# Target one-hots stored in DRAM in one pass of a graph kernel and read back in two later ones

## The chip, the core and the metric

The kernel runs on one core of a Trainium2 chip. Its engines are TensorE (PE, matrix products), VectorE (DVE), ScalarE (ACT), GpSimd (POOL) and SyncE (SP), which here only issues transfers. The metric is the time of one execution in device microseconds, as the median of several runs; lower is better.

## What is computed

Four graph layers run one after the other over 12,500 nodes with 32 features and 212,500 edges sorted by target. Each takes a layer norm and a ReLU of x and adds its sums to x:

```
h = relu(layernorm(x));  x += segment_sum(h_rel[src, type] * w, dst)          # layer 0
h = relu(layernorm(x));  x += relu(h@W0 + T1@W1 + (2*prop(T1) - h)@W2 + b)    # layer 1, T1 = prop(h)
h = relu(layernorm(x));  x += attention messages summed over dst              # layer 2
h = relu(layernorm(x));  x += segment_sum(h[src], dst) / max(degree, 1)       # layer 3
prop(v) = segment_sum(w_hat * v[src], dst)
```

So there are five sums over edges. The code numbers them 0, 1, 2 (the two `prop` of layer 1), 3 (attention) and 4 (the mean of layer 3), and a source's row must reach each edge in all of them.

## The kernel before

**Two ways to fetch a row.** Edges lie in 208 groups of 1,024. In the first way GpSimd gathers the rows of a group with eight indirect DMAs of 128 rows each (`gather_rows`, L709), VectorE weighs them and compares their targets with a window of 80 nodes (`weigh_group`, `compare`, L1997), TensorE sums them by the resulting one-hot (`multiply_group`, L1105), and VectorE adds the window to `big` (`add_group`, L1569), after which the slot (one of four) is free for the next gather (L1563). Sums 0 and 3 do all 208 groups this way.

**The second way** avoids the gather. While sum 0 runs, blocks of four groups are sorted by source into 49 buckets of 256 nodes with up to 128 slots each. In sums 1, 2 and 4, part of the edges goes as blocks: 26, 26 and 34 of them (`BLOCKS`). The text calls these sums pass 1, pass 2 and pass 4. What is left for gathers is 104, 104 and 72 groups, and these are interleaved with the blocks: four groups in each block of passes 1 and 2, two in each block of pass 4 (`HIDDEN`, `UNIT`). With sum 0 and the attention that makes 696 gathered groups, 5,568 indirect DMAs.

A block runs in eight batches (`BATCHES`: 7 buckets, then 6 each). For batch q:
- SP spreads the slots' low source numbers from DRAM over 128 partitions (`spread_lows`, L672, 192 or 224 KB, four buffers, `low_numbers_spread`).
- VectorE compares them with the partition number, two instructions (`compare_sources`, L1787), which gives the one-hot of sources (two buffers).
- TensorE picks the rows of the slots by it (`pick`, L1212 or L1215).
- In pass 4 ScalarE copies the picked rows as bf16 (`pick_block`, L915). In passes 1 and 2 VectorE weighs them (L1838, L1841), and VectorE and ScalarE split them in three bf16 parts (L884, L888, L1850, L1855).
- VectorE makes the one-hot of targets, one instruction of 128x256 for each bucket (`compare_targets`, L1794, 49 for a block, two buffers).
- TensorE sums the slots' rows by it (`send`, L1228), and at the end of a block VectorE adds 256 columns to `big` (`add_block`, L1804 or L1808).

What the target one-hot holds depends on the graph alone (`slot_at`), not on the features, and block i holds the same edges in all three passes. Pass 2 builds in the same loop the table of the attention: TensorE L1331 and L1335, ScalarE L1026 and L1030, and stores of 495 or 544.5 KB each from ScalarE's queue.

**What sets the order.** Each engine's program is written by hand, with semaphores between them. VectorE in step q of passes 1 and 2 does sources q+1, weighs q, makes targets q-1 and finishes the split of q-2; TensorE picks q+3 and sends q. In pass 4 VectorE does sources q+1 and targets q, TensorE picks q+1 and sends q. Targets q wait until send q-2 has ended, sources q until pick q-2 has ended. `carry_wait` adds an instruction whose only work is to hold a wait.

Of the kernel before, what the change touches and what calls it, by code (L numbers as in the profile page):

```python
# [19 lines left out]
BF16 = mybir.dt.bfloat16  # L20
# [4 lines left out]
P = 128  # L25
# [8 lines left out]
CH = 8  # L34
GROUP = CH * P
NG = (E + GROUP - 1) // GROUP
SLOTS = 4
# [9 lines left out]
CAP = P  # L47
# [11 lines left out]
TURNS = {s: n // UNIT[s] for s, n in BLOCKS.items()}  # L59
BEFORE = [0, BLOCKS[1], BLOCKS[1] + BLOCKS[2]]  # L60
# [52 lines left out]
def gnn_kernel(nc, x, src, dst, et16, et86, ew, ew1, w0, comp0, w1, b1, w2, comp2, selfw,  # L113
               a1w, a1b, a2w, a2b, rel, out):
    def scratch(name, shape, dt=F32):
        return nc.dram_tensor(name, shape, dt, kind="Internal").ap()
# [7 lines left out]
    lows_d = scratch("lows_d", (NSB * NBK * CAP,), BF16)  # L124

    ctx = ExitStack()
    with ctx:
# [81 lines left out]
        to_oh = {s: [onehot_piece(s, 2 + j).rearrange("p (k w) -> p k w", w=W2) for j in range(2)] for s in BLOCKS}  # L209
# [194 lines left out]
        s_to = sem("targets_compared")  # L404
# [25 lines left out]
        for s in range(5):  # L430
            sums[s]["gathered"] = sums[1]["gathered"] if s == 4 else [sem(f"sum{s}_gathered_{k}") for k in range(SLOTS)]
        GOT = [0, 0, 0, 0, GROUPS[1] // SLOTS * (16 * CH)]
# [138 lines left out]
        def _(sp):  # L571
# [95 lines left out]
            def spread_lows(h):  # L667

                with sp.Fori(0, BLOCKS[(1, 2, 4)[h]]) as i:
                    for q, (b0, n) in enumerate(BATCHES):  # L670
                        sp.wait_ge(s_from, (BEFORE[h] * NBATCH + q + 1) + i * NBATCH)
                        sp.dma_start(lows[q % RING][:, 0:n * CAP],  # L672
                                     lows_d[bass.ds(i * (NBK * CAP) + b0 * CAP, n * CAP)].partition_broadcast(P)).then_inc(s_bc[q % RING], 16)
# [10 lines left out]
            spread_lows(2)  # L684
# [81 lines left out]
        def _(act):  # L766
# [96 lines left out]
            def pick_and_lay_out(s, h):  # L863
# [64 lines left out]
                if TURNS[s] * SLOTS < GROUPS[s]:  # L928
                    with act.Fori(TURNS[s], GROUPS[s] // SLOTS) as i:
                        for k in range(SLOTS):  # L930
                            lay_out_next(s, i, k)
# [169 lines left out]
        def _(pe):  # L1101
# [90 lines left out]
            def pick_and_sum(s, h):  # L1192
# [25 lines left out]
                def send(i, e, q):  # L1218
                    b0, n = BATCHES[q]
                    if q == 0:  # L1220
                        pe.wait_ge(s_sbadd, (BEFORE[h] + e + 1) + i * UNIT[s])
                        carry_wait(pe)
                    if s == 4:
                        pe.wait_ge(s_to, (e * NBATCH + q + 1) + i * (UNIT[s] * NBATCH))
                        carry_wait(pe)
                    pe.wait_ge(s_slot, ((BEFORE[h] + e) * NBATCH + q + 1) + i * (UNIT[s] * NBATCH))
                    for k in range(n):
                        last = nc.tensor.matmul(block_sums[s][0:SPLIT, 0:W2], slot_rows[q % 2][:, k, :], to_oh[s][q % 2][:, k, :],  # L1228
                                                start=(b0 + k == 0), stop=(b0 + k == NBK - 1))
                    last.then_inc(s_sent, 1)  # L1230
# [260 lines left out]
        def _(dve):  # L1491
# [279 lines left out]
            def pick_and_sum(s, h):  # L1771
# [18 lines left out]
                def compare_targets(i, e, q):  # L1790
                    b0, n = BATCHES[q % NBATCH]
                    dve.wait_ge(s_sent, count(i, e, q, 1))
                    for k in range(n):
                        op = V.tensor_scalar(to_oh[s][q % 2][:, k, :], iota2[:, :], at_f[:, e % UNIT[s], b0 + k:b0 + k + 1], None, ALU.is_equal)  # L1794
                    return op
# [19 lines left out]
                def pick_weighed(i, f, first, last):  # L1815
# [4 lines left out]
                    if first:  # L1820
                        start_block(i, f)
                        dve.drain()
                        compare_sources(i, f, 0)
                    for q in range(NBATCH + ((8 if s == 2 else 4) if last else 0)):
# [20 lines left out]
                        if q == 0 and not first:  # L1845
                            start_block(i, f)
# [25 lines left out]
                def pick_turn(i, f, first, last):  # L1872
                    for e in range(UNIT[s]):
# [20 lines left out]
                step = pick_turn if s == 4 else pick_weighed  # L1894
                step(0, 0, True, False)
                with dve.Fori(0, TURNS[s] - 2) as i:
                    step(i, 1, False, False)
                step(0, TURNS[s] - 1, False, True)
# [460 lines left out]
```

## Time and profile before

| | |
|---|---|
| three runs, us | 7821.56, 7808.33, 7819.74 |
| median, us | 7819.74 |
| profiled execution, span from first to last instruction, us | 10430.0 |
| mean granted clock of TensorE in it, share of 2.4 GHz | 0.597 |

The page gives no total for the profiled execution beside its span. This span is a third longer than the median of the runs that were timed without a profile, so the rows show where work and waits lie and how long an instruction takes, but not directly the time of a stage in a timed run.

How to read the views: a row of grouped instructions has the line, the engine, the operation, output and inputs by name, the shapes and the count; behind the bar stand the busy us, the mean ns of one, and the idle time ahead of them with what ended it. "issue" is idle time that ended for no reason that the profile shows, "remote" one ended by an event of unknown source, a transfer for instance. DVEq is VectorE's sequencer. PE's ends are modelled.

### The profile page before, as it was taken

The numbers are of one execution on the slowest core, as the hardware profiler recorded it, in microseconds if no ns is written. First come the engines' busy times: TensorE is split into PE (matmuls) and PEld (weight loads), VectorE is DVE, ScalarE is ACT, GpSimd is POOL, SyncE is SP. The second block draws the span as 40 slices with busy tenths as digits, with TensorE's granted clock in tenths as the row PEclk, the third lists the DMA queues.
The fourth block names the chain that finished last, engine by engine and source line by source line (L and its number), as shares of the span: only waits on it lengthen the run. The fifth ranks groups of instructions, "written<-read, shape, count | busy, mean of one in ns | idle before, by whom it ended". The sixth has DMA issues, their size and how long they took to land. (4 is left out here: it accounts for less than half of the span.)

```text
span 10430.0 us, 148696 instructions
## 1 busy us (share of the span) xinstructions
PE 5347.8 (51%) x40755; PEld 4389.9 (42%) x40756; DVE 4782.2 (46%) x15556; ACT 2574.5 (25%) x8163; POOL 5362.5 (51%) x5577
## 2 busy tenths in 40 slices
PE   4232322232355666656566555555555555556666
PEld 2121222222244444544444444555555545455555
DVE  4444444454456666544444443333333333346665
ACT  4334333333311111123333333111111111121111
POOL 3565555556465555444444443555555555535554
PEclk8555555555566666656666665555555555557777
DMA  5000000000111111134344343111111111112222
GB/s 130 11 11 11 11 11 11 11 10 11 20 38 39 40 40 40 35 100 140 128 141 140 131 139 117 29 30 29 29 31 30 30 30 30 30 33 61 62 62 52
DMA packets 463914, 542.70 MB, mean 52 GB/s; under 512 B 219393, under 2 KB 373025, under 8 KB 463709
## 3 DMA queue, kind: packets, MB, share of 16 engines
q0 software_dynamic: 178288, 148.77, 8.8%
q1 hardware_dynamic: 228973, 178.17, 6.6%
q10 hardware_dynamic: 56448, 213.62, 5.2%
q14 instruction: 150, 1.23, 0.0%
q8 instruction: 55, 0.90, 0.0%
HBM read 293.47 MB, written 246.66 MB: 52 GB/s over the span
## 5 line engine op out<-in xcount | busy, mean ns | idle before, releaser
L709 POOL DMA_INDIRECT arena<-table,ibuf x3328 | 3144.7, 945 | 2571.7 <-issue 1124.4
L709 POOL DMA_INDIRECT arena<-nodes,ibuf x2240 | 2215.1, 989 | 2387.0 <-DVEq L1563 1532.3
L1105 PE MATMUL ps_agg<-mem_a,arena 128*32 128x80 f32 (+1 forms) x3904 | 513.4, 317 | 801.3 <-DVEq L1550 724.6
L1569 DVE TENSOR_TENSOR big<-big,ps_agg 32x80 f32 (+1 forms) x488 | 113.0, 232 | 1687.6 <-PE ps_agg L1105 857.4
L1105 PE MATMUL ps_agg<-mem_b,arena 128*32 128x80 f32 (+1 forms) x3904 | 543.6, 307 | 667.5 <-DVEq L1550 386.4
L1366 PE MATMUL ps_agg<-tbuf,msg 128*64 128x80 f32 x2496 | 373.5, 344 | 936.4 <-DVE msg L2020 861.6
L1105 PEld LDWEIGHTS ps_agg<-mem_a,arena 128*32 128x32 f32 (+1 forms) x3904 | 453.1, 162 | 864.1 <-DVEq L1550 734.1
L1105 PEld LDWEIGHTS ps_agg<-mem_b,arena 128*32 128x32 f32 (+1 forms) x3904 | 436.1, 154 | 751.6 <-DVEq L1550 411.8
L832 ACT ACTIVATE tbuf<-O,tbuf 128x49 bf16<-128x49 bf16 x2176 | 625.3, 365 | 495.3 <-DVE H L1709 307.3
L1366 PEld LDWEIGHTS ps_agg<-tbuf,msg 128*64 128x64 f32 x2496 | 335.9, 226 | 958.1 <-DVE msg L2020 877.0
L1794 DVE TENSOR_SCALAR tbuf<-iota,at_f 128x256 bf16<-128x256 bf16 x2940 | 621.8, 294 | 105.5 <-remote 85.9
L976 ACT ACTIVATE att<-score 128x8 f32<-128x8 f32 x208 | 43.3, 208 | 2252.5 <-DVE score L2011 2046.8
L1228 PE MATMUL ps_t<-tbuf,mem_b 128*96 128x256 bf16 x1440 | 311.2, 377 | 355.4 <-ACT mem_b L915 143.8
L1787 DVE TENSOR_SCALAR tbuf<-idx_a,pcol 128x896 bf16<-128x896 bf16 x960 | 371.6, 428 | 210.8 <-remote 100.6
L1228 PE MATMUL ps_t<-tbuf,mem_a 128*96 128x256 bf16 x1500 | 285.3, 333 | 346.1 <-issue 140.4
L1361 PE MATMUL ps_h<-yw,mem_b 80*128 80x33 f32 x1664 | 376.9, 403 | 96.3 <-ACT yw L958 96.3
L1361 PEld LDWEIGHTS ps_h<-yw,mem_b 80*128 80x128 f32 x1664 | 362.8, 330 | 115.0 <-ACT yw L958 99.7
L2054 DVE TENSOR_TENSOR big<-big,ps_agg 64x80 f32 x208 | 47.9, 230 | 745.2 <-remote 485.3
L1228 PEld LDWEIGHTS ps_t<-tbuf,mem_b 128*96 128x96 bf16 x1440 | 217.9, 171 | 403.6 <-issue 166.7
L1361 PE MATMUL ps_wide<-yw,mem_b 80*128 80x33 f32 x1680 | 380.6, 403 | 1.2 <-ACT yw L958 1.2
L1361 PEld LDWEIGHTS ps_wide<-yw,mem_b 80*128 80x128 f32 x1680 | 366.3, 330 | 19.1 <-issue 17.8
L884 ACT CAST mem_b<-msg 128x192 bf16<-128x192 f32 x208 | 73.2, 352 | 1210.3 <-PE ps_agg L1228 440.7
(388 smaller groups left out, 12225.4 us busy)
## 6 DMA issues: line engine op xcount, KB each, us to landing
table<-tbuf ACTq DMA_DIRECT2D x294, 544.5 KB
idx_a<-lows_d SPq DMA_DIRECT2D x602, 192.0 KB
arena<-table,ibuf POOLq DMA_INDIRECT x3328
table<-tbuf ACTq DMA_DIRECT2D x98, 495.0 KB
arena<-nodes,ibuf POOLq DMA_INDIRECT x2240
table<-tbuf SPq DMA_DIRECT2D x25, 1024.0 KB, 4.3
idx_a<-lows_d SPq DMA_DIRECT2D x86, 224.0 KB
nodes<-O SPq DMA_DIRECT2D x7, 224.0 KB, 3.0
```

What stands on the lines that cost most here:

```text
L709: nc.gpsimd.indirect_dma_start(out=INTO[s][:, k, c, 0:WIDTH[s]], out_offset=None, in_=TABLE[s], in_offset=bass.IndirectOffsetOnAxis(ap=ibu ...
L832: op = nc.scalar.mul(moved[:, j, 2 + part, :], by_bucket[:, j, :], of)
L884: nc.scalar.copy(slot_rows[b][:, 0:n, 0:D], by_tile(weighed[b][:, 0:n * D])).then_inc(s_high, 1)
L976: nc.scalar.activation(att[:, :], score[:, :], ACT.Tanh).then_inc(attn["tanh"], 1)
L1105: last = nc.tensor.matmul(ps_agg[ROW0[s]:ROW0[s] + CHN[s], 0:WIN], narrow[:, k, c, 0:CHN[s]], onehots[b][:, c, :], start=(c == 0), stop=(c ...
L1228: last = nc.tensor.matmul(block_sums[s][0:SPLIT, 0:W2], slot_rows[q % 2][:, k, :], to_oh[s][q % 2][:, k, :], start=(b0 + k == 0), stop=(b0 ...
L1361: last = nc.tensor.matmul(y_own[b][:, c, :], onehot_t[:, c, :], yw[:, :], start=True, stop=True)
L1366: last = nc.tensor.matmul(ps_agg[0:2 * D, 0:WIN], msg[:, c, :], onehots3[k][:, c, :], start=(c == 0), stop=(c == CH - 1))
L1569: V.tensor_tensor(into, into, ps_agg[r0:r1, 0:WIN], ALU.add)
L1787: op = V.tensor_scalar(from_oh[s][q % 2][:, a, 0:n * CAP], lows[q % RING][:, 0:n * CAP], pcol2[:, a:a + 1], None, ALU.is_equal)
L1794: op = V.tensor_scalar(to_oh[s][q % 2][:, k, :], iota2[:, :], at_f[:, e % UNIT[s], b0 + k:b0 + k + 1], None, ALU.is_equal)
L2054: V.tensor_tensor(into, into, ps_agg[0:2 * D, 0:WIN], ALU.add)
```

## The change

In pass 1 every target one-hot is, beside its use, stored in a new DRAM tensor `targets_d` (26 blocks, 49 x 256 bf16 in each of 128 partitions). In pass 2 and in the first 26 of pass 4's 34 blocks, SP reads it back in place of the comparison. Pass 4's target one-hots get four buffers instead of two, and lie in `O`. SP's program interleaves stores and reads with the spreads. VectorE's program for pass 4 is two loops, one without comparisons (26 blocks) and one with them.

```diff
+KEPT = BLOCKS[1]
+TO_RING = {1: 2, 2: 2, 4: 4}
...
+            def keep_targets(i, f, q):
+                sp.wait_ge(s_made, (f * NBATCH + q + 1) + i * NBATCH)
+                sp.dma_start(kept_rows(i, f, q), to_oh[1][q % 2][:, 0:BATCHES[q][1], :].rearrange("p k w -> p (k w)")).then_inc(s_kept[q % 2], 16)
+            def return_targets(h, i, f, q):
+                s = (1, 2, 4)[h]
+                sp.wait_ge(s_sent, ((BEFORE[h] + f) * NBATCH + q + 3 - TO_RING[s]) + i * NBATCH)
+                sp.dma_start(to_oh[s][q % TO_RING[s]][:, 0:BATCHES[q][1], :].rearrange("p k w -> p (k w)"),
+                             kept_rows(i, f, q)).then_inc(s_there[q % TO_RING[s]], 16)
+            def spread_and_keep():
+                late = 6
+                def block(i, f, first=False):
+                    for q in range(NBATCH):
+                        spread_low(0, i, f, q)
+                        if q >= late:
+                            keep_targets(i, f, q - late)
+                        elif not first:
+                            keep_targets(i, f - 1, q - late + NBATCH)
+            def spread_and_return(h, ahead):
+                def block(i, f, last=False):
+                    for q in range(NBATCH):
+                        if q + ahead < NBATCH:
+                            spread_low(h, i, f, q + ahead)
+                        elif not last:
+                            spread_low(h, i, f + 1, q + ahead - NBATCH)
+                        return_targets(h, i, f, q)
...
-            spread_lows(0)
+            spread_and_keep()
             store_nodes(1, 1, lambda i: ubuf[1][i])
-            spread_lows(1)
+            for j in range(2):
+                sp.wait_ge(s_kept[j], 16 * (KEPT * NBATCH // 2))
+            spread_and_return(1, 5)
...
-            spread_lows(2)
+            spread_and_return(2, 4)
...
+                    if s == 2:
+                        pe.wait_ge(s_there[q % 2], 16 * (e * (NBATCH // 2) + q // 2 + 1) + i * (16 * NBATCH // 2))
+                        carry_wait(pe)
...
+                    if s == 1 and (e > 0 or q > 1):
+                        dve.wait_ge(s_kept[q % 2], 16 * ((e * NBATCH + q) // 2) + i * (16 * NBATCH // 2))
+                        carry_wait(dve)
...
-                        if goes(q - 1):
+                        if s == 1 and goes(q - 1):
                             compare_targets(i, f, q - 1)
...
-                            compare_targets(i, n, q).then_inc(s_to, 1)
+                            if not kept:
+                                compare_targets(i, n, q)
```

SP in pass 1, within a block; before, only spreads stand there (`idx_a` holds the spread numbers, `tbuf` the one-hots):

```order
L671 REGISTER_ALU
L672 ISA [waits sources_compared]
L672 DMA idx_a<-lows_d 128x768
L671 REGISTER_ALU
L672 ISA [waits sources_compared]
L672 DMA idx_a<-lows_d 128x768
```

and now:

```order
L679 REGISTER_ALU
L680 ISA [waits sources_compared]
L680 DMA idx_a<-lows_d 128x768
L690 REGISTER_ALU
L691 ISA [waits targets_onehots_made]
L691 DMA targets_d<-tbuf 128x1536
```

A store of 384 KB stands behind each spread. In passes 2 and 4 a read of `targets_d` (into `H` and into `O`) stands in its place, behind a wait for `slots_rows_summed`.

VectorE in pass 1, one step, before:

```order
L1787 TENSOR_SCALAR tbuf<-idx_a,pcol 128x768
L1838 TENSOR_REDUCE msg<-ps_wide 128x192 [waits slots_rows_picked]
L1841 ISA
L1841 TENSOR_TENSOR msg<-msg,slot_ew 128x192
L1794 TENSOR_SCALAR tbuf<-iota,at_f 128x256 [waits slots_rows_summed]
L1794 TENSOR_SCALAR tbuf<-iota,at_f 128x256 x5
L1850 TENSOR_TENSOR msg<-msg,mem_b 128x192 [waits slots_rows_high_part]
```

and now:

```order
L1859 TENSOR_SCALAR tbuf<-idx_a,pcol 128x768
L1914 TENSOR_REDUCE msg<-ps_wide 128x192 [waits slots_rows_picked]
L1917 TENSOR_TENSOR msg<-msg,slot_ew 128x192
L1869 TENSOR_SCALAR tbuf<-iota,at_f 128x256 [waits slots_rows_summed,targets_onehots_kept_1]
L1869 TENSOR_SCALAR tbuf<-iota,at_f 128x256 x5
L1926 TENSOR_TENSOR msg<-msg,mem_b 128x192 [waits slots_rows_high_part]
```

The comparison has one more condition, that the store of the one-hot two batches earlier has landed.

VectorE in pass 4, the middle of a block, before:

```order
L1784 REGISTER_ALU [waits low_numbers_spread_0]
L1787 TENSOR_SCALAR tbuf<-idx_a,pcol 128x768 [waits slots_rows_picked]
L1787 TENSOR_SCALAR tbuf<-idx_a,pcol 128x768
L1794 TENSOR_SCALAR tbuf<-iota,at_f 128x256 [waits slots_rows_summed]
L1794 TENSOR_SCALAR tbuf<-iota,at_f 128x256 x5
L1784 REGISTER_ALU [waits low_numbers_spread_1]
L1787 TENSOR_SCALAR tbuf<-idx_a,pcol 128x768 [waits slots_rows_picked]
```

and now, in the loop of the blocks that are read back:

```order
L1856 REGISTER_ALU [waits low_numbers_spread_0]
L1859 TENSOR_SCALAR tbuf<-idx_a,pcol 128x768 [waits slots_rows_picked]
L1859 TENSOR_SCALAR tbuf<-idx_a,pcol 128x768
L1856 REGISTER_ALU [waits low_numbers_spread_1]
L1859 TENSOR_SCALAR tbuf<-idx_a,pcol 128x768 [waits slots_rows_picked]
```

The six comparisons and their wait for an earlier send are gone from VectorE.

## Rows read from the trace of the kernel before

**Rows 1.** The profile page: span, busy time of each engine

```profile
span 10430.0 us, 148696 instructions
PE 5347.8 (51%) x40755; PEld 4389.9 (42%) x40756; DVE 4782.2 (46%) x15556; ACT 2574.5 (25%) x8163; POOL 5362.5 (51%) x5577
```

**Rows 2.** Busy time in the five sums: stretch, length, engines, PEclk, DMA share, GB/s

```profile
150.00:2800.00 2650.00, 770.95 (x4760) 561.49 (x4760) 1198.32 (x3386) 943.15 (x3505) 1568.59 (x1658) 0.58 0.08 11
2857.00:4247.00 1390.00, 831.37 (x5842) 664.80 (x5842) 899.61 (x2819) 233.11 (x1014) 813.13 (x832) 0.64 0.18 40
4323.00:6254.00 1931.00, 1135.47 (x13519) 899.33 (x13517) 881.87 (x3185) 611.65 (x1778) 810.43 (x832) 0.63 0.39 126
6384.00:9226.00 2842.00, 1618.86 (x8423) 1449.63 (x8424) 912.68 (x3075) 407.43 (x1080) 1569.45 (x1664) 0.50 0.15 30
9310.00:10374.00 1064.00, 631.25 (x6118) 529.13 (x6118) 632.71 (x2442) 183.64 (x349) 591.50 (x576) 0.75 0.26 60
```

**Rows 3.** Groups of POOL's instructions in the same five stretches, in order

```profile
L709 POOL DMA_INDIRECT arena<-table,ibuf x1658 | 1569.3, 947 | 1081.2 <-issue 502.5 <-DVEq L1563 473.3 <-ACT ibuf L823 105.4
L709 POOL DMA_INDIRECT arena<-nodes,ibuf x832 | 813.1, 977 | 633.7 <-DVEq L1563 342.3 <-issue 233.7 <-DMA nodes<-O 57.8
L709 POOL DMA_INDIRECT arena<-nodes,ibuf x832 | 810.4, 974 | 1196.9 <-DVEq L1563 884.7 <-issue 235.4 <-DMA nodes<-tbuf 76.7
L709 POOL DMA_INDIRECT arena<-table,ibuf x1664 | 1569.7, 943 | 1402.6 <-DVEq L2071 782.2 <-issue 620.3
L709 POOL DMA_INDIRECT arena<-nodes,ibuf x576 | 591.6, 1027 | 556.4 <-DVEq L1563 305.3 <-issue 164.6 <-DMA nodes<-H 84.1
```

**Rows 4.** Timeline of one block of pass 4, TensorE and ScalarE: start, us, instruction

```profile
9798.96 0.67 PE L1215 MATMUL ps_wide<-arena,tbuf 128*128 128x96 bf16 x12
9800.97 0.94 PE L1228 MATMUL ps_t<-tbuf,mem_a 128*96 128x256 bf16 x7 [1.34 <-issue]
9801.74 0.67 PE L1215 MATMUL ps_wide<-arena,tbuf 128*128 128x96 bf16 x12
...
9797.91 0.72 ACT L915 CAST mem_a<-ps_wide 128x672 bf16<-128x672 f32 x1 [1.35 <-PE ps_wide L1215]
9806.55 0.64 ACT L915 CAST mem_b<-ps_wide 128x576 bf16<-128x576 f32 x1 [7.93 <-remote]
```

**Rows 5.** Groups of VectorE's instructions in pass 4, 9450 to 10250 us

```profile
L1794 DVE TENSOR_SCALAR tbuf<-iota,at_f 128x256 bf16<-128x256 bf16 x1298 | 273.6, 291 | 27.5 <-remote 17.8 <-PE ps_t L1228 9.5
L1787 DVE TENSOR_SCALAR tbuf<-idx_a,pcol 128x768 bf16<-128x768 bf16 (+1 forms) x424 | 166.3, 434 | 122.2 <-remote 86.5 <-issue 25.0 <-PE ps_wide L1215 10.6
```

**Rows 6.** The waits of VectorE in pass 2: us in total, times, longest

```profile
DVE big L1569 <- PE ps_agg L1105: 225.1, 80, 4.5
DVE big L1804 <- PE ps_agg L1228: 193.6, 23, 8.6
DVE msg L1841 <- remote: 143.3, 38, 18.6
```

**Rows 7.** Transfers issued in the whole execution: KB each, median us to landing

```profile
table<-tbuf SPq DMA_DIRECT2D x25, 1024.0 KB, 4.3
nodes<-O SPq DMA_DIRECT2D x7, 224.0 KB, 3.0
```

**Rows 8.** Timeline of POOL at the start of pass 4

```profile
9311.27 1.30 POOL L709 DMA_INDIRECT arena<-nodes,ibuf  x1 [0.30 <-issue]
9312.87 0.95 POOL L709 DMA_INDIRECT arena<-nodes,ibuf  x1 [0.30 <-issue]
```

More of the change, by code:

```diff
@@ L59 @@
 TURNS = {s: n // UNIT[s] for s, n in BLOCKS.items()}
+KEPT = BLOCKS[1]
+KEPT_TURNS = KEPT // UNIT[4]
+TO_RING = {1: 2, 2: 2, 4: 4}
+assert BLOCKS[2] == KEPT and KEPT_TURNS * UNIT[4] == KEPT and KEPT_TURNS < TURNS[4]
 BEFORE = [0, BLOCKS[1], BLOCKS[1] + BLOCKS[2]]
@@ L403, in gnn_kernel @@
         s_got = sem("slots_rows_picked")
-        s_to = sem("targets_compared")
+        s_made = sem("targets_onehots_made")
+        s_kept = [sem(f"targets_onehots_kept_{j}") for j in range(2)]
+        s_there = [sem(f"targets_onehots_there_{j}") for j in range(4)]
         s_wgh = sem("slots_rows_weighed")
@@ L430, in gnn_kernel @@
         for s in range(5):
-            sums[s]["gathered"] = sums[1]["gathered"] if s == 4 else [sem(f"sum{s}_gathered_{k}") for k in range(SLOTS)]
-        GOT = [0, 0, 0, 0, GROUPS[1] // SLOTS * (16 * CH)]
+            sums[s]["gathered"] = sums[1]["gathered"] if s in (2, 4) else [sem(f"sum{s}_gathered_{k}") for k in range(SLOTS)]
+        GOT = [0, 0, GROUPS[1] // SLOTS * (16 * CH), 0, (GROUPS[1] + GROUPS[2]) // SLOTS * (16 * CH)]
         TURNED = [0, NB, None, 2 * NB, 3 * NB]
@@ new lines, in spread_and_keep @@
+            def spread_and_keep():
[7 more added lines that the diff above has]
+                            keep_targets(i, f - 1, q - late + NBATCH)
+                block(0, 0, True)
+                with sp.Fori(0, KEPT - 1) as i:
+                    block(i, 1)
+                for q in range(NBATCH - late, NBATCH):
+                    keep_targets(0, KEPT - 1, q)
@@ new lines, in spread_and_return @@
+            def spread_and_return(h, ahead):
[6 more added lines that the diff above has]
+                        return_targets(h, i, f, q)
+                more = BLOCKS[(1, 2, 4)[h]] > KEPT
+                for q in range(ahead):
+                    spread_low(h, 0, 0, q)
+                with sp.Fori(0, KEPT - 1) as i:
+                    block(i, 0)
+                block(0, KEPT - 1, not more)
+                if more:
+                    for q in range(ahead, NBATCH):
+                        spread_low(h, 0, KEPT, q)
+                    with sp.Fori(KEPT + 1, BLOCKS[(1, 2, 4)[h]]) as i:
+                        for q in range(NBATCH):
+                            spread_low(h, i, 0, q)
@@ L928, in pick_and_lay_out @@
                 if TURNS[s] * SLOTS < GROUPS[s]:
-                    with act.Fori(TURNS[s], GROUPS[s] // SLOTS) as i:
+                    for i in range(TURNS[s], GROUPS[s] // SLOTS):
                         for k in range(SLOTS):
@@ L1870, in pick_weighed, with pick_turn @@
                             next_part(dve, varied, normed, norm_pair)
-                def pick_turn(i, f, first, last):
+                def pick_turn(i, f, first, last, kept):
                     for e in range(UNIT[s]):
@@ L1892, in pick_turn @@
                         add_block(i, f * UNIT[s] + UNIT[s] - 1)
[L1894 to L1898, printed above, removed]
+                if s == 4:
+                    pick_turn(0, 0, True, False, True)
+                    with dve.Fori(0, KEPT_TURNS - 1) as i:
+                        pick_turn(i, 1, False, False, True)
+                    with dve.Fori(0, TURNS[s] - 1 - KEPT_TURNS) as i:
+                        pick_turn(i, KEPT_TURNS, False, False, False)
+                    pick_turn(0, TURNS[s] - 1, False, True, False)
+                else:
+                    pick_weighed(0, 0, True, False)
+                    with dve.Fori(0, TURNS[s] - 2) as i:
+                        pick_weighed(i, 1, False, False)
+                    pick_weighed(0, TURNS[s] - 1, False, True)
+                if s == 1:
+                    for j in range(2):
+                        dve.wait_ge(s_kept[j], 16 * (KEPT * NBATCH // 2))
                 if TURNS[s] * SLOTS < GROUPS[s]:
```

37 lines of the change are left out of this document (22 added, 15 removed).

## The prediction

> **What bounds the kernel now.** I read the page first: no engine is busy for more than 51% of the span [rows 1], so a share of busy time says nothing here and the stages have to be taken one by one. The busy time in the five sums comes next [rows 2], and then GpSimd's own group in each of them [rows 3], because every sum runs at the pace of something and GpSimd's 5,568 indirect DMAs go through all of them.
>
> GpSimd's idle time in rows 3 has three kinds. "issue" follows each DMA (0.30 us, [rows 8]) and is there whatever the others do. The waits for a freed slot (DVEq L1563, DVEq L2071) and for row numbers (ACT L823) are time in which GpSimd is ahead and held back by others. The waits for `nodes` lie between sums. The second kind adds up to 473.3 + 105.4 + 342.3 + 884.7 + 782.2 + 305.3 = 2,893 us. Without them the span would be 10,430 - 2,893 = 7,537 us.
>
> The timed runs take 7,820 us. That is 2,610 us less than the profiled execution, and only 283 us more than this 7,537. So if GpSimd's own pace is the same with and without a profile, nearly all of the hold-backs of the trace are absent from a timed run. The timeline shows what they can be [rows 4]. TensorE's pick for the second batch is recorded as ended at 9798.96 + 0.67 = 9799.63 us, yet ScalarE's copy of it starts at 9806.55 us, after 7.93 us that no recorded event ends. The copy has no other work ahead of it. TensorE thus reports late, by several us at a time; I take this for a cost of recording its 81,511 instructions (an inference, since no row shows its cause). VectorE's waits in pass 2 for TensorE's group sums and for the last send of a block [rows 6] are of the same sort.
>
> I therefore take GpSimd as the pace of a timed run, with 283 us of hold-backs left. Its own time for a group is (busy + issue) / groups [rows 3]: pass 1 (813.1 + 233.7) / 104 = 10.07 us, pass 2 10.06, pass 4 (591.6 + 164.6) / 72 = 10.50. For a block that is 40.3, 40.2 and 21.0 us. Beside it [rows 2], for a block: VectorE's busy time is 34.6, 33.9 and 18.6 us, TensorE's 32.0, 43.7 and 18.6. Passes 1 and 4 are covered by GpSimd with little to spare (VectorE's registers, drains and waits are not in the busy time). Pass 2 alone has an engine above it, TensorE, and that is where I expect the larger part of the 283 us.
>
> **The change part by part.**
>
> *Removed.* 49 comparisons for each of 52 blocks. One costs VectorE 273.6 / 1,298 = 0.211 us of its time [rows 5] (they overlap, the 291 ns is its own latency). So VectorE loses 49 x 0.211 = 10.3 us a block, 268 us in each of the two passes. That is the size of the edit, not of its worth.
>
> *Pass 4, 26 blocks.* VectorE falls from 18.6 to 8.3 us beside GpSimd's 21.0. It ceases to matter, but GpSimd doesn't move for that. What it can return are hold-backs: by the share of rows 3, 305.3 / 2,893 of 283 us is 30 us; 26 of 34 blocks hold 23 of them, of which I take 15.
>
> *GpSimd's own instruction.* It takes 943 ns in the attention, 974 in pass 2, 977 in pass 1 and 1,027 in pass 4, where VectorE's bf16 comparisons are densest [rows 3]; single ones take 1.30 us beside others of 0.95 [rows 8]. The excess is 8 x 0.084 = 0.67 us for a group in pass 4 and 8 x 0.031 = 0.25 in pass 2. The target comparisons are 273.6 of the 439.9 us of comparisons [rows 5], 62%. With 52 groups of pass 4 and 104 of pass 2 freed of them: 0.62 x (52 x 0.67 + 104 x 0.25) = 38 us. The bounds are 0 (the excess has another cause, as the gather's table) and 61 (all of it goes).
>
> The Trainium skill (SBUF — State Buffer, "SBUF: two separate sides") says that VectorE in a fast mode that uses both ports and GpSimd lock each other out of a shared pair of ports for a whole instruction, so a GpSimd DMA can wait for descriptors while VectorE works. By that rule the slower rows of passes 1, 2 and 4 are this lock, and the term above is real; without it the sum would be 38 us higher. The trace agrees in its order (943, 974, 1,027 ns) but does not show a lock.
>
> *Pass 2, 26 blocks.* VectorE falls from 33.9 to 23.6 us. TensorE's 43.7 stays, and gains one wait instruction for a send. TensorE and VectorE work in lockstep though (a group needs VectorE's weighing, a send VectorE's split), and shorter steps of VectorE let TensorE start earlier. Of the 283 us I give pass 2 half, 140, more than its 885 / 2,893 share (87), as TensorE's busy time is above GpSimd's there alone. Bounds for what comes back are 0 (TensorE bounds) and 140 (the lockstep bounds); I take 45, a third, because the larger work is untouched.
>
> *Added in pass 1.* Every target comparison waits for the store two batches earlier, with one more instruction (carry_wait). SP issues the store of batch T-2 behind the spread of T+4, which waits for sources T. VectorE does sources T and targets T-2 in step T-1, and targets T in step T+1. The store has two steps, 2 x 40.3 / 8 = 10.1 us. Its price: 224 KB land in 3.0 us and 1,024 KB in 4.3 [rows 7], so 384 KB by a straight line in 3.3 us, and behind a spread of 192 KB at worst twice that. It is hidden, by some 3 us or more; the send that VectorE waits for anyway comes in the same time. The instruction has no row; it moves no data, so a whole comparison of 0.211 us [rows 5] is above it: 0 to 8 x 26 x 0.211 = 44 us of VectorE, under GpSimd's cover where it has any. I take 5. Behind a waiting VectorE would stand the split, and so send, and the next free slot: if the cover were gone, each us of lateness costs up to 208 us.
>
> *Added in pass 2 and 4: the reads.* In pass 2 (two buffers) the read of batch q waits for send q-2 and must be there for send q: two steps, 10.1 us, for 3.3 to 6.6 us. In pass 4 (four buffers) SP issues it when sources q are done, since it stands behind spread q+4. VectorE may run three batches ahead of the sends (sources q+3 need only pick q+1, which stands ahead of send q), so four batches share one latency: (6.6 + some 3 us of pick, sources and issue) / 4 = 2.4 us a batch, against GpSimd's 21.0 / 8 = 2.6. Close, and on the safe side. Two first reads and the last stores stand bare between passes: 5 us.
>
> *Transfers.* Pass 2 moves 126 GB/s at a DMA share of 0.39 over 1,931 us [rows 2]: 753 us of all 16 engines for 243 MB. The reads add 26 x 3.2 MB = 83 MB, by the same rate 257 us, so 1,010 us, just below GpSimd's own 1,046. Nothing is over the limit, but little is left, and reads will queue behind stores of 544.5 KB. The Trainium skill (Trainium Kernel Development and Optimization, "Key Constraints") says that transfers from the SP, ACT and POOL queues all run on the same 16 engines and interleave, so a second queue would be no help; by it the fourth rival below is what to fear. The trace before has no pass in which this load is reached.
>
> *The sum.* -15 (pass 4) - 38 (GpSimd's instruction) - 45 (pass 2) + 5 + 5 = -88 us, 7,820 - 88 = **7,732 us**, 1.1% faster. The profiled execution has the lateness of TensorE's reports in addition, which the change doesn't touch; with the same terms and some more for its larger hold-backs I expect a span of about 10,290 us.
>
> **The rivals.**
> - *VectorE was the bound after all.* If GpSimd's 0.30 us of issue is shorter without a profile, its pace is faster than rows 3 say and the 283 us are more. With 0.15 us, GpSimd has 5,568 x 0.15 = 835 us less, and the hold-backs are 1,118. Then pass 2 and 4 return a good part of 2 x 268 us: some 250 in all, 7,570 us. For it: VectorE's 18.6 busy us of pass 4 become over 20 with its registers and waits. Against: the near match of 7,537 and 7,820. Chance 0.17.
> - *Nothing comes back.* GpSimd paces, the slower instructions have another cause, pass 2 is TensorE's: 0 to 10 us, 7,815 us. The change then only empties VectorE. Chance 0.15.
> - *The other side: reads late in pass 2.* With DMA engines busy for 1,010 of about 1,100 us, a read waits behind two table stores and takes over 10 us. TensorE then stands at send q, the group behind it, VectorE's add, and GpSimd's slot. It decides from the point where a read takes longer than two steps; at 0.8 us late for each of 208 reads it costs 166 us, less 58 of gains elsewhere: 7,930 us. For it: 0.39 of DMA share at a pace a quarter or more slower than a timed run. Against: two steps are long, and the buffers of GpSimd (four slots, over 40 us of work) ride out single late ones. Chance 0.20.
>
> **How the numbers follow.** My forecast has the rest, 0.48, and spans 7,650 to 7,804 us. 0.2% is 16 us, about what a measurement of this kernel can tell from no change. Faster by more: 0.48 + 0.17 = 0.65; within: 0.15; slower: 0.20. The range goes down into the first rival (half of it) and up into the last (a bit under half): 7,590 to 7,860 us.
>
> **What would show it.** In the changed profile: GpSimd's mean for an indirect DMA in pass 4 near 960 ns, in pass 2 near 955, and unchanged in sum 0; its hold-backs (DVEq) smaller in pass 4, hardly in pass 2; VectorE's busy time down by about 268 us in both, and no wait of VectorE in pass 1 for a store. If TensorE waits in pass 2 for a DMA into `H`, or in pass 4 for one into `O`, for more than 1 us a block, the last rival holds. The prediction is wrong on the fast side if passes 2 and 4 together shorten by more than 170 us, which would say that VectorE, not GpSimd, set the pace.

## The result

The changed kernel takes 7,843.4 us (median of six runs, 7,831.3 to 7,850.5), the kernel before 7,820.0 in the same set: a ratio of 1.0028, 95% interval 1.0017 to 1.0040. It is slower by 0.3%, where I forecast 1.1% faster.

The profiled execution of the changed kernel has a span of 7,838.6 us, so it isn't longer than a run timed without a profile. That of before, on which the prediction rests, had 10,430 us [rows 1]. A second profiled execution of before (`before_b` below) had 7,831.2 us. All rows below stand against that one. First the page of it, then the page of the changed kernel:

```profile
span 7831.2 us, 148696 instructions
PE 4877.4 (62%) x40755; PEld 4121.4 (53%) x40756; DVE 4736.0 (60%) x15556; ACT 2544.3 (32%) x8163; POOL 5391.4 (69%) x5577
```

```profile
span 7838.6 us, 148740 instructions
PE 4878.9 (62%) x40755; PEld 4148.0 (53%) x40756; DVE 4227.7 (54%) x12982; ACT 2534.6 (32%) x8163; POOL 5365.9 (68%) x5577
```

VectorE lost 2,574 instructions and 508 us of busy time, and the span didn't move. The groups of POOL in the five sums say where it went. Before (`before_b`):

```profile
L709 POOL DMA_INDIRECT arena<-table,ibuf x1664 | 1589.8, 955 | 599.9 <-issue 496.1 <-DVEq L1587 86.1 <-DVEq L1563 17.4
L709 POOL DMA_INDIRECT arena<-nodes,ibuf x832 | 821.8, 988 | 308.7 <-issue 249.5 <-DMA nodes<-O 55.2 <-DVEq L1563 3.4
L709 POOL DMA_INDIRECT arena<-nodes,ibuf x832 | 815.6, 980 | 554.0 <-DVEq L1563 247.9 <-issue 239.0 <-DMA nodes<-tbuf 67.2
L709 POOL DMA_INDIRECT arena<-table,ibuf x1664 | 1573.7, 946 | 632.9 <-issue 632.9
L709 POOL DMA_INDIRECT arena<-nodes,ibuf x576 | 587.8, 1020 | 240.1 <-issue 172.7 <-DMA nodes<-H 64.7 <-DVEq L1563 2.4
```

And the changed kernel, the answer to [rows 3]:

```profile
L777 POOL DMA_INDIRECT arena<-table,ibuf x1664 | 1578.5, 949 | 601.1 <-issue 496.1 <-DVEq L1659 86.6 <-DVEq L1635 18.4
L777 POOL DMA_INDIRECT arena<-nodes,ibuf x832 | 817.9, 983 | 309.8 <-issue 250.7 <-DMA nodes<-O 55.1 <-DVEq L1635 3.4
L777 POOL DMA_INDIRECT arena<-nodes,ibuf x832 | 816.1, 981 | 459.5 <-issue 247.9 <-DVEq L1635 132.9 <-DMA nodes<-tbuf 78.4
L777 POOL DMA_INDIRECT arena<-table,ibuf x1664 | 1570.2, 944 | 629.2 <-issue 629.2
L777 POOL DMA_INDIRECT arena<-nodes,ibuf x576 | 580.6, 1008 | 369.1 <-issue 165.2 <-DVEq L1635 138.9 <-DMA nodes<-H 64.7
```

The wait for a free slot fell in pass 2 from 247.9 to 132.9 us, and rose in pass 4 from 2.4 to 138.9. The first is the gain, the second a new wait of the same size. The stages themselves, each from the start of GpSimd's first indirect DMA in it to the start of its last, in us (one profiled execution each, in the order of the sets; the experiments are explained below):

| kernel | sum 0 | pass 1 | pass 2 | attention | pass 4 | span |
|---|---|---|---|---|---|---|
| before_b | 2,102.6 | 1,074.4 | 1,301.5 | 2,079.8 | 762.3 | 7,831.2 |
| changed | 2,092.1 | 1,071.6 | 1,196.2 | 2,076.0 | 884.1 | 7,838.6 |
| no_compare | 2,096.8 | 1,070.5 | 1,179.8 | 2,075.8 | 739.8 | 7,671.3 |
| early_reads4 | 2,103.6 | 1,073.7 | 1,205.9 | 2,079.9 | 749.6 | 7,732.5 |
| store_only_b | 2,100.0 | 1,074.0 | 1,396.0 | 2,079.8 | 760.3 | 7,927.7 |
| spreads3 | 2,100.5 | 1,076.0 | 1,214.4 | 2,079.4 | 747.4 | 7,724.5 |
| early_both | 2,096.2 | 1,071.5 | 1,200.7 | 2,075.7 | 749.8 | 7,714.7 |
| padded | 2,096.3 | 1,072.8 | 1,396.9 | 2,076.0 | 759.7 | 7,907.4 |
| reads_twice2 | 2,102.0 | 1,073.4 | 1,229.9 | 2,079.4 | 750.6 | 7,757.6 |

Changed against before_b: pass 2 -105, pass 4 +122, the gap between pass 1 and 2 +11 (GpSimd waits 78.4 us for `nodes` there, not 67.2), the gap behind pass 2 -4, sum 0, pass 1 and attention together -17. Sum +7, as the spans say. The -17 hardly belong to the change: GpSimd's indirect DMA has a median of 0.944 us in some executions and 0.947 in others of one set, whatever the kernel, and `padded`, which stores and reads nothing, has the short stages too (2,096.3, 1,072.8 and 2,076.0). Without them it is +24, and the medians of the runs differ by 23.

What pass 4 waits for, in the changed kernel (engine, line, what it waited for; us in total, times, longest):

```profile
DVE big L1641 <- PE ps_agg L1173: 415.2, 56, 9.2
ACT mem_a L983 <- PE ps_wide L1283: 407.2, 133, 14.9
PE ps_t L1300 <- DMA O<-targets_d: 201.4, 53, 4.6
```

TensorE waits 53 times for a read, once in four batches, 3.8 us each, and VectorE waits 7.4 us each time for TensorE's group product. One turn of this in the timeline of the changed kernel. SP (each pair is a spread and a read):

```profile
7190.18 0.33 SPq L680 DMA_DIRECT2D idx_a<-lows_d  x1
7190.76 0.33 SPq L697 DMA_DIRECT2D O<-targets_d  x1
7199.29 0.33 SPq L680 DMA_DIRECT2D idx_a<-lows_d  x1
7199.87 0.33 SPq L697 DMA_DIRECT2D O<-targets_d  x1
7200.45 0.33 SPq L680 DMA_DIRECT2D idx_a<-lows_d  x1
7201.03 0.33 SPq L697 DMA_DIRECT2D O<-targets_d  x1
```

TensorE, and then VectorE:

```profile
7205.01 1.51 PE L1300 MATMUL ps_t<-O,mem_a 128*96 128x256 bf16 x6 [3.97 <-DMA O<-targets_d]
7206.31 1.17 PE L1283 MATMUL ps_wide<-half_tiles,tbuf 128*128 128x96 bf16 x12
7207.28 1.48 PE L1300 MATMUL ps_t<-O,mem_b 128*96 128x256 bf16 x6
7208.69 2.21 PE L1173 MATMUL ps_agg<-mem_b,arena 128*32 128x80 f32 x16
```

```profile
7197.69 0.23 DVE L1641 TENSOR_TENSOR big<-big,ps_agg 32x80 f32 x1 [7.68 <-PE ps_agg L1173]
7198.38 1.41 DVE L1859 TENSOR_SCALAR tbuf<-idx_a,pcol 128x768 bf16<-128x768 bf16 x4 [0.47 <-PE ps_wide L1283]
...
7211.11 0.22 DVE L1641 TENSOR_TENSOR big<-big,ps_agg 32x80 f32 x1 [8.94 <-PE ps_agg L1173]
```

SP issues nothing from 7190.8 to 7199.3, because the next spread waits for VectorE's comparison of sources. VectorE stands in `add_group` until 7197.69. Then it compares, SP issues the spread and, at 7199.87, the read: 2.2 us. This read lets TensorE go on at 7205.01, 5.1 us later. The group product that VectorE needs stands behind the send that waited, a pick and one more send, and starts at 7208.69, after 3.7 us. With its own 2.2 us and 0.2 us more VectorE goes on at 7211.11. The ring is 13.4 us for four batches, 3.35 us a batch, where GpSimd needs 2.6. It isn't a single case: VectorE waits 51 times for over 3 us in `add_group` in these blocks, and from one such wait to the next pass 11.4 to 14.1 us, the median 13.4.

A part of the ring is TensorE's clock. The same turn in windows (TensorE's busy time first; the granted clock is the third number from the end):

```profile
7198.00:7201.00 3.00, 2.56 (x38) 2.18 (x36) 2.55 (x8) 1.28 (x2) 1.88 (x2) 1.00 0.20 33
7201.00:7205.00 4.00, 0.04 (x1) 0.00 (x0) 1.17 (x3) 0.74 (x2) 3.09 (x4) 0.85 0.97 274
7205.00:7209.00 4.00, 3.99 (x27) 3.49 (x28) 0.00 (x0) 0.64 (x1) 2.98 (x4) 0.50 0.91 325
```

TensorE stands nearly idle for 4 us, and what it does next runs at a clock of 0.50 (1.2 GHz). A send of six products then takes 1.51 us instead of 0.82 at 7197.92, a pick 1.17 instead of 0.68 at 7199.19. The two sends and the pick are 1.8 us longer by these numbers, so at least that much of the 13.4 is the lower clock (an estimate; the group product isn't in it).

### The profile page after: what moved, and what is told of

It reads as the page before. It is cut to its first block and busy times, and to the rows that moved or that the text cites. A ratio compares the mean times of both kernels' runs of the same rounds, so it can differ in the third digit from the quotient of the medians.

```text
span 7838.6 us, 148740 instructions
## 1 busy us (share of the span) xinstructions
PE 4878.9 (62%) x40755; PEld 4148.0 (53%) x40756; DVE 4227.7 (54%) x12982; ACT 2534.6 (32%) x8163; POOL 5365.9 (68%) x5577
## 5 line engine op out<-in xcount | busy, mean ns | idle before, releaser
L1173 PE MATMUL ps_agg<-mem_a,arena 128*32 128x80 f32 (+1 forms) x3904 | 494.0, 308 | 616.8 <-DVEq L1622 555.5
L1173 PEld LDWEIGHTS ps_agg<-mem_a,arena 128*32 128x32 f32 (+1 forms) x3904 | 433.4, 157 | 680.3 <-DVEq L1622 574.2
L1173 PE MATMUL ps_agg<-mem_b,arena 128*32 128x80 f32 (+1 forms) x3904 | 475.0, 301 | 487.0 <-DVEq L1622 459.1
L900 ACT ACTIVATE tbuf<-O,tbuf 128x49 bf16<-128x49 bf16 x2176 | 586.4, 363 | 131.4 <-DVE H L1781 131.4
L1615 DVE TENSOR_TENSOR arena<-arena,ew_s 128x256 f32<-128x256 f32 x416 | 176.7, 425 | 413.8 <-DMA arena<-table,ibuf 396.8
L2090 DVE TENSOR_TENSOR msg<-arena,ps_z 128x256 f32<-128x256 f32 x208 | 87.6, 421 | 553.9 <-DMA arena<-table,ibuf 553.9
L891 ACT COPY ibuf<-idx_a 128x8 int32 (+1 forms) x208 | 40.5, 195 | 900.8 <-DMA arena<-table,ibuf 900.8
L952 ACT CAST mem_a<-msg 128x224 bf16<-128x224 f32 x208 | 74.5, 358 | 775.1 <-PE ps_t L1300 480.0
L1425 PE MATMUL ps_wide<-ident,tbuf 128*80 128x128 f32 x1248 | 297.6, 420 | 0.0
L900 ACT ACTIVATE tbuf<-O 128x49 bf16<-128x49 bf16 x1088 | 293.3, 363 | 0.0
```

The source lines that it names most:

```text
L900: op = nc.scalar.mul(moved[:, j, 2 + part, :], by_bucket[:, j, :], of)
L1173: last = nc.tensor.matmul(ps_agg[ROW0[s]:ROW0[s] + CHN[s], 0:WIN], narrow[:, k, c, 0:CHN[s]], onehots[b][:, c, :], start=(c == 0), stop=(c ...
L1425: nc.tensor.transpose(ps_wide[0:WIN, c // 4, (c % 4) * P:(c % 4 + 1) * P], rows[:, c, :], ident[:, :])
L1615: V.tensor_tensor(rows, rows, by[:, of].unsqueeze(2).to_broadcast([P, CH, D]), ALU.mult)
L2090: V.tensor_tensor(msg[:, :, D:2 * D], gbuf[:, k, :, PAIR:PAIR + D], last_in_ps.unsqueeze(2).to_broadcast([P, CH, D]), ALU.mult)
```

## The experiments

Times are medians; each ratio is to the kernel before in the same set, with its 95% interval.

### First set: parts of the change, on a chip where the kernel takes 10,600 us

**before_again** is the kernel before, unchanged.

> The kernel before, unchanged, for a second profiled execution of it. The first one had a span of 10,430 us, the profiled execution of the changed kernel 7,838.6 us, which is the time of its timed runs. If the long span was a cost of recording TensorE's 81,511 instructions (what I inferred), this one is near 10,400 us again, since both kernels have as many. If it was one disturbed execution, this one has a span near 7,818 us, and its stages can be set against those of the changed kernel: sum 0 2,092 us, pass 1 1,072, pass 2 1,196, attention 2,076, pass 4 884, each from GpSimd's first indirect DMA to its last. I expect the second; sum 0, pass 1 and the attention then equal within 3 us each (GpSimd's pace), and passes 2 and 4 together are some 20 us shorter than the 2,080 us of the changed kernel.

Measured: 10,640 us, before 10,609 (1.0031, 1.0013 to 1.0049, for the same program twice; so 0.3% is no difference in this set), profiled span 10,591.7. Neither of the two cases that I wrote came: the long span is real time, timed and profiled alike. On this chip GpSimd's indirect DMA takes as long as elsewhere (0.947 us), but what waits for TensorE's results starts several us after TensorE's recorded end, as in [rows 4]. The 10,430 us of the rows ahead of the prediction look like such a run: it has the same late starts, but no second run ties it to this chip. Stages: 2,701, 1,405, 1,957, 2,872, 1,101 us.

**store_only**: pass 1 stores, passes 2 and 4 compare.

```diff
-            spread_and_return(1, 5)
+            spread_only(1)
...
-            spread_and_return(2, 4)
+            spread_only(2)
```

> Pass 1 stores the one-hots as in the changed kernel, passes 2 and 4 compare as before; nothing is read back. Theory 'late reads in pass 4' (below): the store is free, 7,815 to 7,830 us, pass 1 within 3 us of before. A rival, that the store or its wait is what costs: pass 1 longer by 10 us or more and the time at 7,840 us.

Measured: 10,681 us, 1.0068 (1.0052 to 1.0084); pass 1 47 us longer, pass 2 14 shorter, the attention 61 longer. On this chip the store isn't free in pass 1, against what I expected.

**read_pass2** reads back in pass 2 alone.

> Pass 1 stores, pass 2 reads back, pass 4 compares as before. Theory 'late reads in pass 4': pass 2 is where something is gained, if anything, so 7,780 to 7,820 us. Theory 'DMA load of pass 2' (the DMA engines are busy for 0.83 of it, and stores of 544.5 KB stand before a read): pass 2 is the loser, 7,840 us or more, and the indirect DMAs or TensorE wait there.

Measured: 10,601 us, 1.0003 (0.9986 to 1.0020); pass 2 is 34 us shorter than in before_again, pass 1 39 us longer.

**read_pass4** reads back in pass 4 alone.

> Pass 1 stores, pass 2 compares as before, pass 4 reads back for 26 of 34 blocks. Theory 'late reads in pass 4': in the trace of the changed kernel TensorE waits in pass 4 for a read into O 53 times for 201 us, because a read is issued behind a spread that waits for VectorE, VectorE waits in add_group for TensorE's group product, and this one is queued behind the send that waits for the read. Then this kernel has the whole loss: 7,840 to 7,870 us, with the same 200 us of waits in pass 4. Theory 'DMA load of pass 2': this kernel is at 7,800 to 7,820 us.

Measured: 10,704 us, 1.0090 (1.0072 to 1.0107); pass 4 is 19 us longer, pass 1 47, the attention 59.

The signs speak for late reads in pass 4 and against a DMA limit in pass 2, but the attention, which no kernel changed, is some 60 us longer in two of the three, more than what is looked for. I draw no price from this set.

### Second set, on a chip where it takes 7,836 us

**before_b**, unchanged.

> The kernel before, unchanged, once more. In the first set of runs it took 10,609 us, timed and profiled alike, and 7,820 us in the runs that the change was timed with: so the long span isn't a cost of recording, it is that of the chip on which a run falls. If this set falls on a chip where it takes 7,820 us, its profile gives the stages that the changed kernel's (7,838.6 us) are to be compared with: I expect sum 0 2,092, pass 1 1,055 to 1,072, pass 2 1,180 to 1,220, attention 2,076 and pass 4 840 to 880 us. If it falls on one of 10,600 us, the stages are as before: 2,701, 1,405, 1,957, 2,872, 1,101.

Measured: 7,837.0 against 7,835.5 us (1.0001, 0.9989 to 1.0013). Pass 2 is longer than I expected, 1,301 us, and pass 4 shorter, 762: pass 4 was at GpSimd's pace already.

**no_compare**:

```diff
-                        if goes(q - 1):
+                        if (s == 1 or first) and goes(q - 1):
                             compare_targets(i, f, q - 1)
...
-                            compare_targets(i, n, q).then_inc(s_to, 1)
```

> The kernel before, which leaves out nearly all target comparisons of passes 2 and 4 (8 batches are made at the start of pass 2, two at the start of pass 4) and stores and reads nothing: TensorE multiplies by the one-hots that lie in the buffers, so the sums of both passes are others. It is what the change would bring if storing and reading cost nothing at all. My prediction has 98 us for it on a chip of 7,820 us (38 + 45 + 15): 7,722. Theory 'the comparisons are worth little, GpSimd and TensorE pace': under 30 us. Theory 'the gain is there and the reads give it back': 60 us or more.

Measured: 7,684.1 us, 0.9814 (0.9797 to 0.9830). My three terms had 98 us for this kernel. With nothing stored or read, leaving out the comparisons gives 151 us: 122 in pass 2, 23 in pass 4.

**early_reads4**:

```diff
-            spread_and_return(2, 4)
+            spread_and_return(2, 2)
```

> The changed kernel, but in pass 4 the spreads run two batches ahead of the reads instead of four, so that a read of batch q stands behind the spread of q+2, which waits for sources q-2, and no longer behind sources q; its own condition, send q-4, is then the last. Theory 'late reads in pass 4' (a read is issued only when VectorE gets to sources q, which stands behind add_group, which stands behind the group product and the send that wait for the read): TensorE's 201 us of waits for reads into O nearly vanish and pass 4 gets 30 to 80 us shorter than the 884 us of the changed kernel. Rival, that the reads are late because they take 5.8 us and the DMA engines are the limit: within 10 us of the changed kernel.

Measured: 7,729.2 us, 0.9864 (0.9847 to 0.9881). Pass 4 went from 884 to 750 us by the order of SP's issues alone; the reads, their size and their buffers are the same. The waits in pass 4 of this kernel:

```profile
DVE mem_a L2084 <- DMA arena<-nodes,ibuf: 183.1, 33, 7.8
DVE big L1641 <- PE ps_agg L1173: 43.6, 45, 2.9
PE ps_t L1300 <- DMA O<-targets_d: 17.6, 22, 1.7
```

TensorE's wait for reads fell from 201.4 to 17.6 us, VectorE's for TensorE from 415.2 to 43.6, and VectorE now waits for what GpSimd gathers. The theory of late reads holds, and gives more than the 30 to 80 us that I expected of it; that 5.8 us of landing or the DMA engines were the limit doesn't hold: the same reads go through a shorter pass, at a DMA share of 0.67 instead of 0.55.

**store_only_b**, the same kernel as store_only.

> Pass 1 stores, nothing is read back, as in the first set, where pass 1 took 1,451 us against 1,405 of before and the whole was 0.7% slower on a chip of 10,609 us. If the store costs in pass 1 on a chip of 7,820 us too, pass 1 is 10 us or more longer than that of the kernel before in the same set; if GpSimd covers it there, both are within 5 us.

Measured: 7,931.0 us, 1.0128 (1.0111 to 1.0144). Pass 1 has 1,074.0 against 1,074.4 us: the store and its wait cost nothing there. But pass 2, whose code is that of before, has 1,396 against 1,301.5. In its trace VectorE stands for 2.8 us at each jump back to the start of pass 2's loop; 0.3 us in before_b. The two places, store_only_b first:

```profile
4091.81 0.21 DVE L2081 SCALAR_TENSOR_TENSOR O<-tcent,tdev 128x64 f32 x1
4094.98 0.75 DVE L1863 TENSOR_SCALAR H<-idx_a,pcol 128x768 bf16<-128x768 bf16 x2 [2.96 <-issue]
```

```profile
4099.50 0.21 DVE L1993 SCALAR_TENSOR_TENSOR O<-tcent,tdev 128x64 f32 x1
4100.18 0.79 DVE L1787 TENSOR_SCALAR H<-idx_a,pcol 128x768 bf16<-128x768 bf16 x2 [0.46 <-issue]
```

### Third set, 7,837 us

**spreads3**:

```diff
-            spread_and_return(2, 4)
+            spread_and_return(2, 3)
```

> The changed kernel with the spreads of pass 4 three batches ahead of the reads, between the four of the changed kernel and the two of the last set (which made the whole 1.4% faster than before and pass 4 750 us long instead of 884). A read then stands behind the spread that waits for sources q-1, one VectorE step earlier. Theory 'late reads in pass 4', by which the lateness of a read is that of VectorE: pass 4 lies between, 760 to 840 us, and TensorE's waits for reads into O are a fraction of the 201 us. If one step is enough, it is as with two, 750 us.

Measured: 7,722.3 us, 0.9844 (0.9825 to 0.9864), pass 4 747.4 us. Not between: one step is enough. TensorE still waits 101.7 us for reads, but GpSimd waits only 1.2 us for slots in pass 4, so the ring is no longer slower than GpSimd.

**early_both**, with a wait that keeps the first read off `H` until pass 1 is done with it:

```diff
+                if h == 1:
+                    sp.wait_ge(s_from, BEFORE[h] * NBATCH + RING + 1)
...
-            spread_and_return(1, 5)
+            spread_and_return(1, 3)
...
-            spread_and_return(2, 4)
+            spread_and_return(2, 2)
```

> As in the last set with two batches in pass 4, and in pass 2 the spreads three batches ahead of the reads instead of five. In pass 2 a read must in any case wait for send q-2, since there are two buffers. If the reads of pass 2 are late because of the spread ahead of them, pass 2 goes from 1,196 to 1,206 us towards the 1,180 of the kernel without comparisons and reads; if they aren't, it stays within 5 us, 7,725 to 7,735 us in all.

Measured: 7,716.1 us, 0.9843 (0.9827 to 0.9860), pass 2 1,200.7 us. Pass 2 is within 5 us of the changed kernel's and TensorE waits 0.2 us for `H` in it: there the reads weren't late for their place in the queue. The whole is 9 us below the range that I gave, and level with spreads3; both are faster than the kernel before, and the changed one is slower than it.

**padded**: the kernel before with 28 drains ahead of pass 2's loop.

```diff
+                    for _ in range(28):
+                        dve.drain()
```

> The kernel before, with 28 drains of VectorE ahead of the loop of pass 2, which do nothing. With stores alone, pass 2 took 95 us longer than before in the last set, though its own code is the same; in its trace VectorE needs 2.8 us for each jump back to the start of that loop and 0.3 in the kernel before, and the loop begins 28 instructions later in VectorE's program. If the place of the loop is the cause, this kernel is as slow: 1.0 to 1.3% slower than before, jumps of 2.8 us in pass 2. If the stores are, it stays at the time of before.

Measured: 7,923.4 us, 1.0114 (1.0096 to 1.0131), pass 2 1,396.9 us, jumps of 2.8 us. The stores are cleared; it is the place of the loop. The profile also shows what comes with it. It lists the DMA queues that load instructions (packets, MB, share); one of them in pass 2, before_b (3442 to 4745 us) and then padded (3433 to 4830 us):

```profile
q14 instruction: 9, 0.07, 0.0%
```

```profile
q14 instruction: 124, 1.02, 0.2%
```

In padded and in store_only_b five such loads of 8 KB come for each turn of pass 2's loop, in before_b none. After each of the 23 jumps one starts 1.0 to 1.8 us behind the branch and ends at 1.5 (median), and VectorE goes on at 2.8 or 2.9. The profile doesn't say whose instructions they are; their place says VectorE's. A turn with all its parts takes 56.6 us in padded and 52.5 in before_b, and 23 times these 4.1 us are 94 of the 95: 2.6 us lie in the jump, 2.0 more come in the first 17 us of the turn, and 0.5 are won back by its end.

**reads_twice2**:

```diff
+                if s == 2:
+                    sp.dma_start(copy_d[bass.ds(i * P + f * P, P), BATCHES[q][0] * W2:(BATCHES[q][0] + BATCHES[q][1]) * W2],
+                                 kept_rows(i, f, q)).then_inc(s_there[q % 2], 16)
```

> As in the last set with two batches in pass 4; ahead of each read of pass 2 the same 384 KB are also copied from DRAM to another DRAM tensor, and the send waits for both. It doubles the transfers that the change added to pass 2, where the DMA engines were busy for 0.83. Rival 'reads late in pass 2' with its mechanism right and only its point not reached: pass 2 gets longer by 50 us or more and TensorE waits for H; if the transfers have room, within 10 us of 1,206.

Measured: 7,754.2 us, 0.9890 (0.9874 to 0.9907). Pass 2 has 1,230 us, 24 more than early_reads4: GpSimd waits 167.6 us for a slot in it instead of 145.6, TensorE 10.0 us for `H` instead of none. Neither of the two cases. Pass 2 in windows, early_reads4 and then this kernel (PEclk, DMA share and GB/s at the end):

```profile
3453.00:4661.00 1208.00, 893.98 (x13610) 758.45 (x13611) 636.97 (x1936) 594.74 (x1789) 816.48 (x832) 0.81 0.82 269
```

```profile
3451.00:4682.00 1231.00, 914.58 (x13606) 775.79 (x13606) 635.78 (x1935) 594.64 (x1787) 819.46 (x832) 0.79 0.95 329
```

Even at a DMA share of 0.95 the pass is only 2% longer: no cliff up to there, but a price.

## Why the prediction failed, step by step

**The step that failed** is in "Added in pass 2 and 4: the reads": "VectorE may run three batches ahead of the sends [...] so four batches share one latency: [...] 2.4 us a batch, against GpSimd's 21.0 / 8 = 2.6. Close, and on the safe side." I counted what `compare_sources` waits for, and left out what stands ahead of it on VectorE. `add_group` waits for a group product that stands on TensorE behind a send, and that send waits for the read whose issue waits, by SP's order, for `compare_sources`. The four batches do share one latency, as I wrote, but it holds the read, two sends, a pick and the group product: 13.4 us, not 9.6. The read was well sized (5.1 to 5.8 us for up to 6.6); the "some 3 us of pick, sources and issue" are 8.3. The forecast had this ring on the safe side by 0.2 us a batch, and it was 0.75 us over. It costs 884 - 750 = 134 us. The sign that I named under "What would show it", "TensorE waits [...] in pass 4 for one into `O`, for more than 1 us a block", is what the profile shows (201.4 / 26 = 7.7 us), but the rival that it was meant for isn't: early_reads4 has the same transfers in less time and loses nothing.

**"TensorE thus reports late [...] a cost of recording"**: wrong. Profiled and timed runs are equally long, in the set of 10,600 us and in the others. The inference built on it held all the same outside pass 2: GpSimd paces. In before_b its waits for slots are 17.4 + 3.4 + 247.9 + 0 + 2.4 = 271 us (I had 283 of hold-backs), and 86.1 in sum 0 for another step of VectorE. Their places were wrong: I took them from the shares of the long trace and gave pass 2 half; nearly all are pass 2's, and pass 2 is the one sum that GpSimd doesn't pace.

**Pass 2, -45**: the mechanism was right, the size less than half: -105. I took a third of 140 us "because the larger work is untouched"; of 247 us over GpSimd's own time (1,301.5 less 815.6 + 239.0) 105 came back, and 122 with no reads at all. The jumps of its loop take 0.3 us in before_b, in the changed kernel and in no_compare, so the place of the loop has no part in this. TensorE wasn't above GpSimd either: its busy time is 953.7 / 26 = 36.7 us a block here, not 43.7.

**Pass 4's hold-backs, -15**: there were none to give back (2.4 us). The sign that I named, fewer of them in pass 4 and hardly fewer in pass 2, came the other way round: 138.9 for 2.4 us, and 132.9 for 247.9.

**GpSimd's own instruction, -38** (22 in pass 4, 16 in pass 2): about right in pass 4 and wrong in pass 2. The groups of POOL in the stretch of pass 4 whose blocks are read back, before_b and then early_reads4:

```profile
L709 POOL DMA_INDIRECT arena<-nodes,ibuf x394 | 405.7, 1030 | 120.3 <-issue 118.7 <-DVEq L1563 1.2 <-ACT ibuf L823 0.3
```

```profile
L777 POOL DMA_INDIRECT arena<-nodes,ibuf x417 | 413.0, 990 | 127.3 <-issue 125.7 <-ACT ibuf L891 1.2 <-DVEq L1635 0.3
```

40 ns less for each of 416, 17 us, of which the pass shows 13; without any target comparison it is 984 ns. In pass 2 the mean is 980 ns before, 981 changed and 989 in no_compare. So the target comparisons aren't what makes pass 2's instruction longer than the attention's 946 ns. The lock of which the Trainium skill speaks (SBUF — State Buffer, "SBUF: two separate sides") may be what pass 4 shows, and in pass 2 the comparisons of sources, which stay in every kernel, may hold it; no run here shows the lock itself.

**Pass 1, +5**: 0 (store_only_b). **Between passes, +5**: +11 against before_b, in GpSimd's wait for `nodes` ahead of pass 2. It scatters: this wait is 67.4 to 78.9 us in the kernels that store and read, and 64.6 to 72.2 in those without reads.

**Reads late in pass 2 (0.20)**, which the prediction once calls the fourth rival and lists as the third: didn't come. TensorE has no wait for `H` in the changed kernel's pass 2; reads and load cost 16 us (1,196.2 against the 1,179.8 of no_compare), and twice the added load another 24. The time is slower than before, as this rival had it, but by another pass and another mechanism. The Trainium skill says that the queues of SP, ACT and POOL all run on the same 16 DMA engines (Trainium Kernel Development and Optimization, "Key Constraints"). The profile agrees in that it counts three queues over the same 16 in pass 2 (40.6, 34.4 and 8.1%, together the 0.83); no run here shows how they interleave.

With the ring out of the way (early_reads4) the profiled span is 99 us shorter than that of before_b: pass 2 -96, pass 4 -13, the gap ahead of pass 2 +9, the rest +1; the timed runs say -106. The sum that I forecast was -88, but its near match is luck, since errors of size cancel in it: pass 2 was worth twice my term, GpSimd's instruction a third of it. It is no proof of the sum.

**Open**: which places of a loop bring the instruction loads wasn't tried beyond these two. What holds pass 2 at 1,180 us without its target comparisons, 112 above GpSimd's own 822.9 + 245.1, wasn't tried either. Nor is it settled why what follows TensorE comes late in one set.

## What to carry to other kernels

When a wait moves from one engine to a queue, walk the whole ring: what the issuing queue waits for, what stands ahead of that on its engine, and what stands ahead of that in turn. A prefetch should hang on its own buffer alone; behind another transfer in the same queue it inherits that one's wait. And look whether the profile's span is that of the timed runs before taking shares of stages from it: if they differ, the stages are another run's.

## What was not expected of the hardware

- **TensorE's clock behind a short wait.** In the changed pass 4 the granted clock is 0.50 while TensorE works off what stood behind a wait of 4 us for a read, and 1.00 ahead of it (7198 to 7209 us above). So a late transfer costs its own lateness and slower products behind it.
- **The place of a loop.** VectorE's loop of pass 2 in the kernel before (282 recorded instructions a turn) needs 0.3 us for each jump back, and 2.8 us where 28 instructions stand ahead of it (padded); in store_only_b as well. The same loop, 95 us in the end, and five loads of instructions for each turn where there were none. The shorter loops, of pass 1 (210 or 223) and of the changed pass 2 (231), have 0.3 in these kernels; the longer one of sum 0 (367 or 371) has 3.0 in all, and about six loads for each turn. A kernel that differs only in code ahead of such a loop can be 1.1% slower, and a comparison of variants should look for it: the instruction queues in the profile's DMA view tell.
- **The chip.** The same program took 10,609 us in one set and 7,836 in two others, each set on a chip of its own (three in all). GpSimd's instruction lasts as long; what differs is when the engines that wait for TensorE go on. That the chip makes the difference, and not something else in that set, isn't shown, since each chip ran one set. One kernel cost +0.7% in the set of 10,609 us (store_only) and +1.3% in one of 7,836 (store_only_b): its slow jumps in pass 2 are there in both, but only in the second do they lengthen the pass.
- **A small step.** The median indirect DMA is 0.944 or 0.947 us, by the execution. For 5,568 of them that is 17 us, 0.2% of the whole and nearly as much as the change's 0.3%.
